# Transposing the next sequence's combine weights one expert later in a mixture-of-experts kernel

## What is computed

```
x = _layernorm(x + _L0_attn_ref(x, w_q, w_k, w_v, w_o))      # 16 heads, softmax over 512 keys
router_logits = jnp.einsum('bsd,de->bse', x, gate_w)         # 8 experts
top_logits, top_idx = jax.lax.top_k(router_logits, 2)
top_w = jax.nn.softmax(top_logits, axis=-1)
combine = jnp.sum(one_hot(top_idx, 8) * top_w[..., None], axis=-2)
h = jax.nn.silu(jnp.einsum('bsd,edf->ebsf', x, w1))          # 128 -> 256
y = jnp.einsum('ebsf,efd->ebsd', h, w2)                      # 256 -> 128
x = _layernorm(x + jnp.einsum('ebsd,bse->bsd', y, combine))
```

## Time and profile before

| | before |
|---|---|
| median of 3 runs | 1280.31 us |
| lowest and highest run | 1279.3 and 1281.87 us |
| profiled execution, first to last instruction (span) | 1280.0 us |
| TensorE busy | 1196.7 us, 93% of the span |
| VectorE busy | 987.7 us, 77% |
| GpSimd busy | 679.6 us, 53% |
| ScalarE busy | 602.0 us, 47% |
| mean granted TensorE clock | 0.978 of full speed |

### The profile page before, as it was taken

One profiled execution on the slowest core, in us unless ns is written; L12 is line 12 of the kernel. 1 busy time (PEld: TensorE's weight loads), 2 busy tenths in 40 slices (PEclk: granted clock), 3 DMA queues, 4 the chain that ended last, 5 costly groups with the idle time before them and its releaser, 6 DMA issues. The chain is left out here.

```text
span 1280.0 us, 20247 instructions
## 1 busy us (share of the span) xinstructions
PE 1196.7 (93%) x4952; PEld 693.9 (54%) x4952; DVE 987.7 (77%) x1618; ACT 602.0 (47%) x744; POOL 679.6 (53%) x502
## 2 busy tenths in 40 slices
PE   5799999999999999999999999999998788888886
PEld 3454555555555555555555555555553566666664
DVE  4586888788888788888788888788887667777764
ACT  4444444444444444444444444444443555556553
POOL 0464644455544455544555544555546366666665
PEclk9898999999999999999999999999999889999999
DMA  9666666566665565665666665656660000000000
GB/s 213 162 161 153 157 155 157 144 156 147 157 156 140 144 155 146 158 159 153 150 150 153 159 148 140 150 149 152 160 161 21 21 9 17 17 17 16 8 9 17
DMA packets 91643, 153.47 MB, mean 120 GB/s; under 512 B 18016, under 2 KB 36960, under 8 KB 91616
## 3 DMA queue, kind: packets, MB, share of 16 engines
q1 hardware_dynamic: 91616, 153.14, 48.1%
HBM read 6.30 MB, written 2.10 MB: 7 GB/s over the span
## 5 line engine op out<-in xcount | busy, mean ns | idle before, releaser
L1025 DVE TENSOR_REDUCE neg_max<-psum 128x1 fp32r<-128x512 f32 x512 | 345.1, 680 | 114.1 <-PE psum L530 112.1
L1040 DVE RECIPROCAL zT<-zT 128x128 f32<-128x128 f32 x256 | 241.4, 944 | 4.2 <-ACT zT L865 2.2
L530 PE MATMUL psum<-k_stack,q_stack 128*128 128x512 f32 x512 | 224.6, 451 | 6.8 <-DVE neg_max L1025 1.4
L555 PE MATMUL psum<-q_stack,k_stack 128*128 128x512 f32 x512 | 210.5, 411 | 9.9 <-DMA q_stack<-q_stack 7.4
L858 ACT ACTIVATE probs_even<-psum 128x1024 f32<-128x1024 f32 x128 | 131.0, 1023 | 179.1 <-PE psum L556 179.1
L556 PE MATMUL psum<-q_stack,k_stack 65*128 65x512 f32 x512 | 205.2, 401 | 0.0
L396 POOL TENSOR_TENSOR probs_sum<-probs_even 128x512 f32<-128x512 f32 x64 | 82.5, 1289 | 227.4 <-PE psum L581 187.2
L396 POOL TENSOR_TENSOR probs_sum<-x_tok 128x512 f32<-128x512 f32 x64 | 82.2, 1284 | 226.9 <-PE psum L581 226.9
L530 PEld LDWEIGHTS psum<-k_stack,q_stack 128*128 128x128 f32 x512 | 97.1, 190 | 185.0 <-DVE neg_max L1025 87.9
L396 POOL TENSOR_TENSOR probs_sum<-probs_sum,probs_even 128x512 f32<-128x512 f32 x128 | 164.1, 1282 | 14.5 <-ACT probs_even L858 3.3
L396 POOL TENSOR_TENSOR probs_sum<-probs_sum,x_tok 128x512 f32<-128x512 f32 x128 | 164.3, 1283 | 11.3
(11 more groups left out here) (119 smaller groups left out, 1927.1 us busy)
## 6 DMA issues: line engine op xcount, KB each, us to landing
q_stack<-q_pair SPq DMA_DIRECT2D x128, 256.0 KB, 3.0
k_stack<-k_pair SPq DMA_DIRECT2D x128, 256.0 KB, 3.6
q_stack<-q_pair SPq DMA_DIRECT2D x128, 128.0 KB, 3.5
k_stack<-k_pair SPq DMA_DIRECT2D x128, 128.0 KB, 3.4
xT_cur<-xT SPq DMA_DIRECT2D x32, 512.0 KB, 3.0
wqk_cur<-w_tab SPq DMA_DIRECT2D x63, 256.0 KB, 3.3
wo_cur<-w_tab SPq DMA_DIRECT2D x64, 128.0 KB, 3.0
x_tok<-L_attn_x_dram SPq DMA_DIRECT2D x8, 256.0 KB, 5.4
```

What stands on the lines that cost most here:

```text
L530: nc.tensor.matmul(psum[:, COARSE + t % 2, :], q_stack[j][:, h, 0, t * P:(t + 1) * P], k_stack[j][:, h, 0, :], start=True, stop=True).then ...
L555: nc.tensor.matmul(psum[:, t, :], k_stack[j][:, h, 0, keys], q_stack[j][:, h, 0, :], start=True, stop=False)
L1025: nc.vector.tensor_reduce(neg_max[h][:, t:t + 1], psum[:, COARSE + t % 2, :], AX.X, ALU.max, negate=True).then_inc(s["max_done"], 1)
L1040: nc.vector.reciprocal(zT[:, cols], zT[:, cols]).then_inc(s["r_done"], 1)
```

## The change

The transposition of the combine weights of sequence b + 1 on TensorE, and both readings of it, on ScalarE and on VectorE, are issued in step 4 in place of step 3. Nothing else is changed: the same instructions with the same waits are issued.

```diff
@@ tensor, chunk(b, j) @@
-                        if e == 3:
+                        if e == 4:
                             transpose_c(b + 1)
```

## The result

The changed kernel is slower: 1299.25 us median (1297.86 to 1299.85), against 1281.09 us for the kernel before in the same comparison. The ratio is 1.0136, with a 95% interval of 1.012 to 1.0152. The forecast was slower, 1287.3 us, with a range to 1296: the direction was right and the size was not. I had 7 us; it is 18 us. The profiled execution has a span of 1297.4 us, against 1280.0.

The account below looks back on a forecast made before the run. TensorE, busy 93% of the span, was taken as the bound. Sequences 1 to 5 cost 1.5 us each for the clock (+7.5), sequence 0 0, sequence 6 -0.5: +7.0 us, 1287.3 us, range 1278 to 1296.

Parts of the forecast that it names:

- The bound, and what the change removes: TensorE, busy 93% of the span, no longer waits in step 3; seven sequences had lost 4.0 us in the gap, 1.7 behind.
- The gap moves to `spread_c` of expert 7: TensorE waits there for VectorE's gating of expert 6: a gap of 3.8 us, where it was 3.98 us.
- the list of signs: What the changed trace would show: line 706's wait gone, seven waits at line 725, six of about 1.5 us at line 679.
- The second gap at `to_tokens`: After the transposes TensorE waits for both readings, about 1.5 us, which eats what step 3 has gained.
- The lower end of my times: VectorE's reading ends at 1101.9, so `to_tokens` starts at 1101.95; the upper value was 1102.4.
- `to_tokens` at the same time as before: Next sequence's `hidden` of expert 0, the step after `to_tokens`, starts at about 1102.6 in both kernels, taken as 0 change.
- The clock, 1.5 us per sequence: Half clock reaches into TensorE's work behind the second gap: 1.5 us taken, from 0 to 3.4 us.
- The sign that the sequences 1 to 5 follow each other at about 36 us: In the changed trace these sequences were to be spaced about 36 us, in place of 34.3.
- the clock that costs no more than now: Rival, chance 0.22: the gaps move but half clock costs nothing more; 1275.3 to 1283 us.
- more is lost: Rival, chance 0.06: the slow stretch is double and filled with work in nearly every sequence; 19 us, 1299 us.
- a gap that closes: Rival, chance 0.05: `spread_c` of expert 7 need not wait, and 40 us go in seven sequences; 1240 us.
- VectorE's short operations end with GpSimd's subtractions: Rule for lines 1177 and 1185, 2.27 and 1.83 us: they exclude GpSimd's SBUF reads and wait; the sum stays as is.

## Why the prediction was right in direction and wrong in size

- **The bound, and what the change removes**: right. The wait for line 1185 is gone in sequences 0 to 6, and `hidden` and `second` run in its place.
- **The gap moves to `spread_c` of expert 7**: right, 3.68 us measured in sequence 2, 3.8 forecast. It is 3.6 to 3.7 us in sequences 1 to 6, but 2.40 in sequence 0, whose gating comes earlier; the list of signs had asked for seven waits of 3.5 to 3.9 us. The run with the statistics behind the gating shows the cause: 1.3 us less ahead of it, 1.3 us less gap.
- **The second gap at `to_tokens`**: right in size (1.48 us, forecast about 1.5), and wrong in part in what sets it. The lower end of my times had VectorE's gating and ScalarE's high part on the path. The upper end had transposes at half clock, ScalarE, VectorE, and the run with only the transposition moved shows that this is the chain.
- **`to_tokens` at the same time as before (-0.3 to +0.2 us, taken as 0)**: right at full clock only. With both gaps filled it starts 9.65 us behind `spread_c` of expert 6 (1102.12 - 1092.47), where it was 9.52 us before. In the changed kernel it is 10.08 us (1106.04 - 1095.96). `spread_c` and the transposes ran at half clock there: 0.60 us from the start of `spread_c` to the transposes in place of 0.24, and four transposes in 1.05 us, where those of line 679 took 0.60.
- **The clock, 1.5 us per sequence**: this is the step that failed, and it is the size of the term that was wrong. I took the cost of a single slow stretch, 3.4 us, nearer than that of a double one. Measured in sequences 2 to 5 was a stretch of 10.2 us, longer than the double one that I had taken as the longest. The work behind `to_tokens` alone lost about 2.5 us (5.74 us from `to_tokens` to the next `spread_c`, 1106.04 to 1111.78, where it was 3.21 us before by the timeline of the same place). I had bounded the term at 3.4 us but held the upper part to be unlikely, although showed a long stretch where there was only short work. My reason was also wrong as a reading: not all seven gaps before show the single stretch. The one of sequence 0 has 6.8 us at half clock, 4.0 us of them filled with work.

The run with both gaps filled splits the loss into the prediction's own two terms, by the same times from `spread_c` to `spread_c` as in the table above:

| sequence | 0 | 1 | 2 | 3 | 4 | 5 | 6 |
|---|---|---|---|---|---|---|---|
| changed kernel, both gaps filled, us | 11.64 | 12.83 | 12.91 | 12.90 | 12.90 | 12.89 | 10.44 |
| gaps: that less before | -1.3 | +0.1 | +0.2 | +0.3 | +0.3 | +0.4 | -1.7 |
| forecast | -1.5 | 0 | 0 | 0 | 0 | 0 | -2.0 |
| clock: changed kernel less that | 2.0 | 2.3 | 2.9 | 3.0 | 3.0 | 3.1 | 2.6 |
| forecast | 1.5 | 1.5 | 1.5 | 1.5 | 1.5 | 1.5 | 1.5 |

The gaps sum to -1.8 us, forecast -3.5. The clock sums to 18.9 us, forecast 10.5. So 8.4 of the missing 10.1 us are the clock's term.

- **The sign that the sequences 1 to 5 follow each other at about 36 us**: measured 36.6 us for sequence 1 and 37.4 to 37.5 for the others.
- **The rivals**: the clock that costs no more than now is what the run with the first gap filled looks like (1282.5 us). The number that came true is that of "more is lost", to which I had given 0.06, at 1299 us. Its mechanism came true only in part, and the match to the microsecond is luck: it has a double stretch filled with work, and measured was a triple one with some 3 us of idle time in it (7.0 to 7.3 us of work in 10.2). The rival on the other side, a gap that closes, did not come: the run with `to_tokens` in step 5 still has the first gap, and 2.3 of the 5 us that it gains on the kernel before lie in sequence 0, where that gap is 2.4 us. That VectorE's short operations end with GpSimd's subtractions held in the changed kernel, where nothing moved, and in the run with `route2` behind the gating, where it did.

In short: 7 us of the loss are there at full clock too, 1.6 to 1.7 us in each of sequences 1 to 5, and 10 us are the half clock that two gaps in a row prolong.

## What to carry to other kernels

A wait that is moved back on the busiest engine lands on the next wait that its delay has hidden, here two of them; list all waits between the old and the new place, with the time at which each would be met, before counting a gain. A short gap behind a long one can cost more through TensorE's clock than by its length: price the stretch at half clock by its longest case wherever work between two gaps is short, and allow for one longer than any that the trace before shows, as the 10.2 us here. Look also for what follows the moved step directly: moving `to_tokens` along, which is worth nothing by itself, turned a loss of 18 us into a gain of 5, and with the statistics moved too into one of 15.

## What the runs showed of the hardware that I had not expected

The granted clock stayed at 1.2 GHz for 10.2 us across a burst of 1.6 us of matmuls and a gap of 1.5 us, and through some 5 us of unbroken matmuls behind it. Sixteen matmuls without use in each of the seven gaps of 4 us made the kernel before 9 us faster (1272.9 against 1281.8). The Trainium skill, "TensorE: Matmul & The Clock Gate", section "HAM oscillation — how this bites in real kernels", describes a wait of 3 to 5 us that comes back with every tile and puts the clock down every time. The trace agrees in the kernel before and in the changed one, with seven of seven sequences. It does not agree for every gap of such a length: with the second gap filled, the clock did not fall behind the gap of 3.58 us in sequence 1. Nor does a shorter gap always leave the clock up: a single gap of 2.4 us lowered it in two of seven sequences, and one of 1.7 us in two of six.

VectorE's short operations of lines 1177 and 1185 take 0.19 us each ahead of sequence 0, where GpSimd is idle. When they start inside a GpSimd subtraction, they end with it, and take 2.27 and 1.83 us. The addition of line 1234 (128x512) grew for a like reason, from 0.80 us in the kernel before to 1.36 us in the changed one. In both it ends 0.55 us behind the end of such a subtraction, but it started 0.8 us ahead of that end and not 0.2 us. TensorE then waited up to 0.7 us for line 1146 behind it, but the two steps around that wait did not get longer: 8.33 us in the changed kernel, 8.42 before.
